# A mixture of experts with attention on one core: 8 weights and 8 expert numbers at the end of a row in place of 64 weights

## The reference, cut to what matters

```python
x = x + 0.5 * ffn(layernorm(x))
x = x + attention(layernorm(x))
x = x + 0.5 * ffn(layernorm(x))

def ffn(x):                                   # TOPK, CAP = 6, 256; E, H, HS = 64, 64, 128
    y_s, g_s = split(x @ w_shared_up)
    shared = silu(g_s) * y_s @ w_shared_down
    scores = sigmoid(x @ w_gate)              # one per expert, 64
    _, topk_idx = top_k(scores, TOPK)
    w = take_along_axis(scores, topk_idx)
    w = w / w.sum(-1, keepdims=True)
    # the first 256 rows that chose an expert are its own
    g_r, v_r = split(x_disp @ w_up[e])        # 512 -> 2 x 64, per expert
    out_r = (silu(g_r) * v_r) @ w_down[e]     # 64 -> 512
    routed = sum over the row's 6 experts of w * out_r
    return shared + routed
```

## Time and profile before

| | us |
|---|---|
| median of 3 runs (lowest, highest) | 3377.15 (3371.05, 3379.41) |
| the profiled execution's own time | 3358.77 |
| its span, first to last instruction | 3357.0 |
| `route`, first | 0 to 197 |
| `experts`, first (last scatter issued) | 197 to 609 |
| `attention` | 609 to about 2680 |
| `route`, second | about 2680 to 2868 |
| `experts`, second (last scatter issued) | 2868 to 3277 |
| `combine` | 3277 to 3357 |

### The profile page before, as it was taken

The page is one execution under the profiler, slowest core; times in us unless marked ns, Lnnn a source line. Parts: engine busy times, 40 slices in busy tenths (PEclk is TensorE's granted clock), DMA queues, the critical chain, the costliest instruction groups (busy, mean ns, idle before and its releaser), DMA issues. The chain is left out here.

```text
span 3357.0 us, 50764 instructions
## 1 busy us (share of the span) xinstructions
PE 2909.1 (87%) x15136; PEld 1560.1 (46%) x15136; DVE 2040.3 (61%) x3891; ACT 1517.1 (45%) x2846; POOL 2206.9 (66%) x1386
## 2 busy tenths in 40 slices
PE   7977777398999999999999999999999889778760
PEld 4644444275444454444444444444444355444430
DVE  7943222476787677677776776776777188322222
ACT  3422222252666565566565655655665444222220
POOL 2158887440888687687787876876877511688870
PEclk9988988697999999999999999999999999888885
DMA  5579999782576667575766666665756343899998
GB/s 212 191 221 242 245 234 227 209 287 92 110 164 133 140 138 144 124 152 118 161 132 128 151 134 141 138 139 125 151 111 149 90 146 120 245 242 233 244 197 310
DMA packets 217009, 576.34 MB, mean 172 GB/s; under 512 B 33948, under 2 KB 34972, under 8 KB 192792
## 3 DMA queue, kind: packets, MB, share of 16 engines
q0 software_dynamic: 84128, 337.69, 50.1%
q1 hardware_dynamic: 128376, 226.84, 20.6%
q10 hardware_dynamic: 4224, 8.39, 0.6%
HBM read 230.94 MB, written 155.24 MB: 115 GB/s over the span
## 5 line engine op out<-in xcount | busy, mean ns | idle before, releaser
L1670 DVE TENSOR_REDUCE attention_mx<-attention_pM 128x1 f32<-128x512 f32 x1984 | 1210.2, 680 | 346.5 <-PE attention_pM L1514 338.5
L1451 ACT ACTIVATE attention_prob<-attention_pS 128x512 f32<-128x512 f32 x2048 | 1060.1, 618 | 609.6 <-PE attention_pS L1501 568.6
L1392 POOL TENSOR_TENSOR attention_pair<-attention_prob 128x1024 f32<-128x1024 f32 x380 | 948.8, 2502 | 269.8 <-ACT attention_prob L1451 265.4
L1514 PE MATMUL attention_pM<-prep_kT,attention_qT 96*128 96x512 f32 x1984 | 877.9, 445 | 0.0
L1501 PE MATMUL attention_pS<-attention_qT,prep_kT 128*128 128x512 f32 x2048 | 841.6, 417 | 24.4 <-issue 17.1
L1501 PEld LDWEIGHTS attention_pS<-attention_qT,prep_kT 128*128 128x128 f32 x2048 | 389.7, 191 | 289.2 <-issue 178.8
L1514 PEld LDWEIGHTS attention_pM<-prep_kT,attention_qT 96*128 96x128 f32 x1984 | 374.2, 190 | 312.0 <-DVE attention_mx L1670 244.3
L1549 PE MATMUL attention_pO<-attention_prob,attention_v 128*32 128x512 f32 x4096 | 492.4, 598 | 0.0
L629 POOL DMA_INDIRECT sum<-experts_res,c_table x256 | 403.3, 1575 | 89.7 <-issue 68.3
L755 DVE TENSOR_SCALAR experts_res<-experts_pD,experts_rows 128x512 f32<-128x512 f32 x128 | 90.8, 746 | 480.0 <-DMA sum<-experts_res,c_table 474.0
L658 PE MATMUL experts_pT<-c_ident,experts_rows 128*128 128x128 f32 x1024 | 184.2, 319 | 188.3 <-DVE experts_xT L739 139.3
(11 more groups left out here) (163 smaller groups left out, 2730.3 us busy)
## 6 DMA issues: line engine op xcount, KB each, us to landing
prep_acc<-attention_pair POOLq DMA_DIRECT2D x96, 1024.0 KB, 7.6
attention_acc<-attention_pair POOLq DMA_DIRECT2D x90, 1024.0 KB, 7.8
experts_wup<-in_L_ffn_w_up_dram SPq DMA_DIRECT2D x128, 256.0 KB, 5.2
attention_qT<-q_parts SPq DMA_DIRECT2D x96, 256.0 KB, 6.6
xn_rows<-route_xn SPq DMA_DIRECT2D x16, 1152.0 KB, 6.3
sum<-route_sh SPq DMA_DIRECT2D x16, 1024.0 KB, 4.4
experts_wdn<-in_L_ffn_w_down_dram SPq DMA_DIRECT2D x64, 256.0 KB, 5.8
attentionp_got<-sum SPq DMA_DIRECT2D x16, 1024.0 KB, 9.1
```

The source lines that it names most:

```text
L1392: pool.tensor_tensor(to[:, part], prob[2 * n % PROBS][:, part], prob[(2 * n + 1) % PROBS][:, part], ALU.add).then_inc(s_pair, 1)
L1451: act.activation(prob[t % PROBS][:, h * QT:(h + 1) * QT], pS[:, at, :], ACT.Exp).then_inc(s_ex, 1)
L1514: pe.matmul(pM[:, r % 3, :], qT[g][0:3 * DH, h, t * P:(t + 1) * P], kT[0:3 * DH, key:key + 512], start=True, stop=True).then_inc(s_mp, 1)
L1670: dve.tensor_reduce(mx[:, unit, part:part + 1], pM[:, r % 3, :], X, ALU.max).then_inc(s_mr, 1)
```

## The change

A row of `xn` now ends with 16 numbers in place of 64: the 8 best scores of the row times half the reciprocal of the weight sum (only the first 6 are used), and the 8 expert numbers. A row is 528 numbers, 2112 bytes. `own` leaves `route`. In `experts` DVE makes, for each pair, the four columns of weights: it compares the six expert numbers with the expert's own number, multiplies with the six weights, and sums the six. Those columns, in `wt`, take the place of the column of `rows` for ACT and DVE.

```diff
+PICKS = 8
+ROW = C + 2 * PICKS
-ROW = C + E
...
-                    dve.tensor_tensor(own[:, :, :], sc[i % 3][:, :, :], mask[:, :, :], ALU.mult).then_inc(s_sel, 1)
+                    dve.tensor_copy(xn[:, i % RING, :, C + PICKS:ROW], i8f[:, :, :]).then_inc(s_sel, 1)
...
-                    dve.scalar_tensor_tensor(xn[:, i % RING, :, C:ROW], own[:, :, :], 0.5,
-                                             wrec[:, :].unsqueeze(2).to_broadcast([P, TURN, E]), ALU.mult, ALU.mult
+                    dve.scalar_tensor_tensor(xn[:, i % RING, :, C:C + PICKS], v8[:, :, :], 0.5,
+                                             wrec[:, :].unsqueeze(2).to_broadcast([P, TURN, PICKS]), ALU.mult, ALU.mult
...
+        own = m.sb("own", [P, Q, TOPK])
+        wt = [m.sb(f"wt{b}", [P, Q]) for b in range(2)]
...
-                    act.wait_ge(s_g[e % RING], (e // RING + 1) * (16 * Q))
+                    act.wait_ge(s_wt, A + e + 1)
...
-                                       scale=rows[e % RING][:, h, C + 2 * e:C + 2 * e + 1]).then_inc(s_ea, 1)
+                                       scale=wt[e % 2][:, h:h + 1]).then_inc(s_ea, 1)
...
-                    dve.wait_ge(s_g[e % RING], (e // RING + 1) * (16 * Q))
+                    dve.wait_ge(s_wt, A + e + 1)
...
+                def weights(e):
+                    dve.wait_ge(s_g[e % RING], (e // RING + 1) * (16 * Q))
+                    dve.wait_ge(s_wt, A + e)
+                    for a in range(2):
+                        own_rows = rows[e % RING][:, a * HALVES:(a + 1) * HALVES, :]
+                        dve.scalar_tensor_tensor(own[:, a * HALVES:(a + 1) * HALVES, :], own_rows[:, :, C + PICKS:C + PICKS + TOPK],
+                                                 float(2 * e + a), own_rows[:, :, C:C + TOPK], ALU.is_equal, ALU.mult
+                                                 ).then_inc(s_own, 1)
+                    dve.wait_ge(s_own, A + 2 * (e + 1))
+
+                    dve.wait_ge(s_ea, A + (e - 1) * HALVES)
+                    dve.tensor_reduce(wt[e % 2][:, :], own[:, :, :], X, ALU.add).then_inc(s_wt, 1)
...
                         gathered(e, 1)
+                        weights(e)
                     if there(e - 1):
                         weighted(e - 1)
```

More of the change, by code:

```diff
@@ L159, in route @@
         cum = m.sb("cum", [P, E], BF16)
-        own = m.sb("own", [P, TURN, E])
         count = m.sb("count", [P, TURN, E])
@@ L580, in experts @@
         s_hid = m.sem("hid")
+        s_own = m.sem("own")
+        s_wt = m.sem("wt")
         s_dn = m.sems("dn", 2)
@@ L733, in _ @@
             def _(dve):
-                begin(dve, s_cd, s_gs, s_hid, s_ed)
+                begin(dve, s_cd, s_gs, s_hid, s_ed, s_own, s_wt)
                 def gathered(e, a):
@@ L755, in weighted @@
                         dve.tensor_scalar(res[e % 2][:, 1, h, :], pD[:, h, 1, :],
-                                          rows[e % RING][:, HALVES + h, C + 2 * e + 1:C + 2 * e + 2], None, ALU.mult
-                                          ).then_inc(s_ed, 1)
+                                          wt[e % 2][:, HALVES + h:HALVES + h + 1], None, ALU.mult).then_inc(s_ed, 1)
+                def weights(e):
[9 more added lines that the diff above has]
+                    dve.tensor_reduce(wt[e % 2][:, :], own[:, :, :], X, ALU.add).then_inc(s_wt, 1)
                 for e in range(PAIRS + 1):
```

## The result

| us | before | with the change |
|---|---|---|
| median of 22 runs each | 3375.08 (3370.80 to 3380.58) | 3370.12 (3367.14 to 3375.66) |
| ratio, 95% interval | | 0.9986 (0.9980 to 0.9992) |
| profiled execution | 3358.77 | 3372.09 |

The change is 5.0 us faster, 0.14%, with an interval from 2.7 to 6.8 us. That is half of the 0.3% that one comparison of a few runs can tell from nothing; 22 runs a side tell it. The two profiled executions say the opposite, by 13 us, which is the first thing to explain.

A forecast was written before the change was run, and what follows sets the result against it. The prediction took POOL's issuing to bound `experts` and DVE to bound `route`. Terms of -3.5, +3.0 and -0.5 us made -1.0, so 3376 us from a median of 3377.15, range 3358 to 3394.

The forecast's parts named there:

- POOL's issuing is the bound of `experts`: In `experts`, 4 gathers, 4 scatters and 0.30 us gaps on POOL fill the whole pair period of about 12.6 us.
- Rival 2: In `experts` the DMA engines are the bound, so fewer gather bytes save 26 us: 3350 us; chance 0.12.
- `route`, -3.5 us: Smaller DVE instructions in `route` gain 0.44 us a turn, kept in turns 2 to 5 of both stages.
- One sign in the prediction: In `route`, L440 x4 still taking 4.7 us would show that only 0.28 us a turn arrived.
- the 1.16 us of the first stage: DVE's wait behind turn 6 of `route`, hanging on the mask: there the gain only lengthens the wait.
- Bytes at the start of a stage, -0.5 us: Smaller gathers land earlier before PE's first transposes in `experts`: 0.25 us for each stage.
- DVE's own account, 0: In `experts` three more DVE instructions a pair, some 0.45 us, are hidden in DVE's slack: 0.
- POOL's hold by DVE, +3 us: In `experts` 128 two-operand DVE instructions hold POOL 0.05 us each, 0.56 us lost per us: +3 us, bounds 1 to 10.
- Rival 1: In `experts` each two-operand DVE instruction costs POOL its whole record, 0.17 to 0.18 us, or 0.28: 3396 or 3409; chance 0.14.
- Rival 3: None of `route`'s gain arrives, as DVE's L440 always ends with POOL's L270: 3380 us; with the forecast, chance 0.74.
- the forecast of -1.0: Whole kernel: the terms for `route`, POOL's hold and the gathers' bytes sum to 1.0 us less, called "same"; chance of same 0.73.
- The base of the absolute number: Whole kernel: terms summed on the profiled execution of 3358.8 us, 18.4 under the median, then applied to the median 3377.15.

## Why the prediction was right, and where it was not

**The bound.** "POOL's issuing is the bound of `experts`" held: rows of 2112, 2304 and 2816 bytes give the same time, 0.9986, 0.9984 and 0.9983 of before, and what made POOL's issues longer made the kernel slower. Rival 2 and its 26 us fall. What the Trainium skill, *DMA: Bandwidth & Descriptors*, on how a descriptor splits into AXI transactions, says of reads that start off a multiple of 256 bytes could not be tested here, since there was no gain from bytes for it to take from.

**`route`, -3.5 us.** The mechanism was right and the term too small; one turn is missing from it. In turns 2 to 5 it went as worked out: the steps fell by 0.25 us each, and the second L440 came ahead of POOL's L270. From L440 of turn 2 to that of turn 6 it is 84.9 us before and 83.2 after, 1.7 us for four turns where 1.76 was the term. (One sign in the prediction was wrong: L440 still takes 4.71 us, and yet the whole 0.5 arrived and not 0.28, because its start and its end move together.)

Behind turn 6 the prediction took the 1.16 us of the first stage as a wait that swallows the gain, and held the second stage to be the same. It isn't. From the sixth mask (L483) to the seventh it is 19.5 us in that first stage, but 21.1 to 21.2 in the second and in both stages of the second profile of before. In all 22 `route` stages of the change (two profiles) and of the nine kernels made from it that keep DVE's order in `route`, it is 19.5 to 19.7. The rows that tell them apart, PE and DVE, second stage of before and first stage after, with the stretch of PE's counting and up product (the third number from the end is the granted clock):

```profile
2810.70 0.24 PE L321 MATMUL route_pP<-route_mask,c_tri 128*128 128x64 bf16 x1 [2.29 <-DVE route_mask L483]
2811.44 5.02 PE L297 MATMUL route_pG<-route_xT,route_wsu 128*128 128x512 f32 x8
2819.99 0.69 DVE L451 TENSOR_TENSOR route_hs<-route_gs,route_pH 128x512 f32<-128x512 f32 x1 [2.17 <-PE route_pH L297]
...
2810.70:2816.29 5.59, 5.59 (x22) 2.85 (x23) 5.59 (x7) 3.49 (x6) 3.12 (x1) 0.69 0.94 347
```

```profile
139.11 0.20 PE L321 MATMUL route_pP<-route_mask,c_tri 128*128 128x64 bf16 x1 [1.80 <-DVE route_mask L483]
139.53 3.68 PE L297 MATMUL route_pG<-route_xT,route_wsu 128*128 128x512 f32 x8
146.73 0.69 DVE L451 TENSOR_TENSOR route_hs<-route_gs,route_pH 128x512 f32<-128x512 f32 x1 [1.65 <-issue]
...
139.10:143.04 3.94, 3.93 (x22) 2.03 (x23) 3.94 (x6) 3.31 (x6) 2.66 (x1) 1.00 1.03 384
```

Before, PE stood still for 2.29 us until DVE's mask, then ran its next matmuls at a granted clock of 0.69, part of the time at 1.2 GHz and part at 2.4, and DVE waited for the product. With the change the pause is 1.80 us, since DVE's chain is 0.5 us shorter, and the clock stays at 2.4 GHz. So the edit saved about 1.6 us more in that turn, in three of the four stages of before. That the shorter pause is what keeps the clock up is argued and not shown: in the second profile of before a pause of 2.29 us was followed by a product of 3.68 us, at the full clock, and in the first profile of either kernel one of 1.72 by a product of 5.22 and 4.89 us.

Together, from the first mask to the eighth, a stage of `route` takes 146.0 us in the mean before (144.8 to 146.4) and 143.1 with the change (142.8 to 143.4): 2.8 us a stage, **5.7 us** in place of 3.5. The run with `route`'s edits alone has the same, 3374.73 - 3369.03 = 5.7.

The profile of before that the prediction had was an odd one in its first stage twice over: its turn 6 was short, and the 24 matmuls of L334 at its end were slow, by the stretches that hold them alone (before, then the change; the second number is PE's busy time, the third from the end the granted clock):

```profile
187.40:192.80 5.40, 5.28 (x24) 3.33 (x24) 3.46 (x19) 0.00 (x0) 0.00 (x0) 0.51 0.74 195
```

```profile
185.70:190.10 4.40, 4.26 (x24) 2.91 (x24) 3.48 (x19) 0.00 (x0) 0.00 (x0) 0.65 0.82 214
```

In both PE had stood still for 4.4 us until DVE's L509. A clock of 0.51 is the lower level, 1.2 GHz, nearly throughout; 0.65 is a mixture. In the other three stages of before these matmuls took 4.26 us as after, so this 1.0 us is not the change's doing.

**Bytes at the start of a stage, -0.5 us.** From the first gather to PE's first transposes it was 10.6 to 11.3 us in eight stages with 2304 bytes and 9.6 to 11.0 in eighteen with 2112, means 10.9 and 10.4: 0.5 a stage, twice the term. None of it shows in the time (rows of 2304 bytes give 0.9984, of 2112 0.9984 and 0.9986); in the executions with the standstill POOL waits 9 to 12 us behind it.

**DVE's own account, 0.** Held: L759 still sat idle for 8.6 us, no engine but ACT waited for `wt` (1.0 us in the first profile of the change, 3.2 in the second).

**POOL's hold by DVE, +3 us.** This is the term that was wrong in size: it measures 0. The step that failed is the proportion: I took 0.56 us lost for each us of hold from two instructions of 0.7 and 2.3 us and applied it to a hold of 0.05 us that I gave each of the tiny ones, themselves 0.16. 640 tiny ones cost nothing that shows, 64 of 0.69 us cost 0.13 us each. Rival 1, the whole record, falls with it. The Trainium skill's *SBUF — State Buffer*, on the two sides of SBUF and their doors, states that the loser is fully blocked, where DVE has two inputs in SBUF and the GpSimd instruction reads SBUF; it also tells of a `tensor_tensor` that did not stall DMAs issued from GpSimd. The runs agree with neither: for the long instruction, a `tensor_tensor`, they show POOL held by a fifth of DVE's time, and for the tiny ones no hold shows. For DVE's side the rule agrees: one L440, usually 0.54 us, takes up to 3447 ns beside L270 after the change as well.

**Rival 3**, that nothing of `route`'s gain arrives, falls with the turns above.

**The sum.** With 0 for POOL's hold, 0 for the bytes and -5.7 for `route` it is -5.7 us, and -5.0 was measured (interval -2.7 to -6.8). So the forecast of -1.0 was right in kind and in range, and 4 us short; both terms that were off, the hold and the missing turn, erred to the same side, and the forecast of "same" held because both were small beside 0.3%. The base of the absolute number was a weak one: the one profiled execution that I summed against had neither stage's standstill.

## What to carry to other kernels

Where two resources look full, take the period of the one with a queue apart, instruction by instruction and gap by gap: if durations and gaps are constant and fill the period, it is the bound, and a DMA share near 1.0 beside it says nothing. Two small instructions on the engine that bounds a stage were worth more than 8% of a gather's bytes behind one that does not. Where the same stage runs twice, read a wait in both before you let it swallow a gain: here the one stage read was the odd one out of four. If an engine stands still beside another's instruction, look which of its own instructions run there unhindered, and put those there.

## What the runs showed of the hardware that was not expected

- The DMA share stayed at 1.02 to 1.03 from 233 to 261 GB/s in the same stage.
- A gain on DVE came with one of PE's clock: behind a pause of 1.8 us the up product took 3.68 us at full clock, behind one of 2.3 us it took 5.02 at 0.69, and the turn took 19.5 us in 22 stages of 22 with the change and in one of four before. What keeps the clock up is not shown.
- Near the start of `experts` ACT waited 13 to 15 us for what it got after 6.6 us in the profile without a standstill, with the wait laid to "remote"; SP resumes with it. It costs POOL about 9 us a stage, comes in whole series of runs (before at 3374.73 and 3378.41 us) and is absent from another (3359.59). Its cause is open.
- Tiny DVE instructions with two operands in SBUF (0.16 us) cost POOL's issuing nothing; one of 0.69 us costs it 0.13 us.
